# Carried sums of a grouped softmax kept in PSUM: the carry is multiplied bank to bank, and a ninth identity product goes

## The reference

```python
w_m = (efeat @ W_msg + b_msg).reshape(E, in_f, -1)
w_a = (efeat @ W_attn + b_attn).reshape(E, in_f, -1)
h_src = feat[src][:, :, None]
e1 = w_m * h_src                       # values, 16 x 16 an edge
e2 = w_a * h_src                       # scores, 16 x 16 an edge
seg_max = jax.ops.segment_max(e2, dst, num_segments=N)
ex = jnp.exp(e2 - seg_max[dst])
denom = jax.ops.segment_sum(ex, dst, num_segments=N)
ft = jax.ops.segment_sum(e1 * (ex / denom[dst]), dst, num_segments=N)
return ft.sum(axis=1)                  # then residual and layer norm
```

## Time and profile before

| | |
|---|---|
| median of 3 runs | 5913.23 us (5909.15 to 5915.31) |
| the profiled execution's own time | 5915.26 us |
| its span, first to last instruction | 5913.5 us |
| VectorE busy over the span | 5183.5 us (88%) |
| TensorE, GpSimd, ScalarE busy | 4496.4 (76%), 4372.5 (74%), 2455.9 us (42%) |
| granted TensorE clock, mean of the span | 0.899 |

### The profile page before, as it was taken

One profiled execution on the slowest core, in us unless ns is written; L12 is line 12 of the kernel. 1 busy time (PEld: TensorE's weight loads), 2 busy tenths in 40 slices (PEclk: granted clock), 3 DMA queues, 4 the chain that ended last, 5 costly groups with the idle time before them and its releaser, 6 DMA issues. The chain is left out here.

```text
span 5913.5 us, 71022 instructions
## 1 busy us (share of the span) xinstructions
PE 4496.4 (76%) x17923; PEld 2168.9 (37%) x17923; DVE 5183.5 (88%) x8909; ACT 2455.9 (42%) x4460; POOL 4372.5 (74%) x4105
## 2 busy tenths in 40 slices
PE   1178887887878878678888888888888888888880
PEld 1044444444444444333333333333333333333330
DVE  5378787787877878699999999999999999999996
ACT  1022222222222222155555555555555555555553
POOL 6677777777777777277777777777777777777762
PEclk6599999999999999889999999999999999989995
DMA  4133333333333333111111111111111111111113
GB/s 134 47 92 92 96 96 93 99 92 94 87 77 77 76 78 76 30 26 27 27 27 27 27 27 27 27 27 27 26 26 27 27 27 27 27 27 27 27 21 114
DMA packets 335266, 315.22 MB, mean 53 GB/s; under 512 B 190903, under 2 KB 274576, under 8 KB 334977
## 3 DMA queue, kind: packets, MB, share of 16 engines
q0 software_dynamic: 156096, 199.34, 14.9%
q1 hardware_dynamic: 179137, 115.52, 7.2%
HBM read 220.82 MB, written 168.57 MB: 66 GB/s over the span
## 5 line engine op out<-in xcount | busy, mean ns | idle before, releaser
L1020 POOL DMA_INDIRECT xg<-x1tab,edge x1920 | 1976.2, 1029 | 585.2 <-issue 583.7
L787 PE MATMUL pagg<-ohh,stt 128*128 128x512 bf16 x4704 | 1702.6, 401 | 458.9 <-DVE ohh L707 458.7
L654 POOL DMA_INDIRECT bg<-btab,mt x1568 | 1683.2, 1073 | 479.6 <-issue 476.3
L1091 PE MATMUL ps<-work,ident 128*128 128x512 f32 x3840 | 1942.7, 630 | 0.2 <-DVE work L1179 0.2
L788 PE MATMUL pagg<-ohh,stt 128*128 128x270 bf16 x4704 | 1370.9, 291 | 0.0
L1140 DVE TENSOR_TENSOR work<-pw,xg 128x1024 f32<-128x1024 f32 x960 | 1112.5, 1210 | 21.3 <-DMA xg<-x1tab,edge 21.3
L1080 PE MATMUL pw<-w,et 99*128 99x512 bf16 x1920 | 680.1, 441 | 574.3 <-DVE work L1140 568.5
L1091 PEld LDWEIGHTS ps<-work,ident 128*128 128x128 f32 x3840 | 779.6, 203 | 725.4 <-issue 632.3
L1063 ACT ACTIVATE work<-work,mt 128x256 f32<-128x256 f32 x1920 | 861.5, 500 | 131.3 <-DVE work L1140 109.2
L787 PEld LDWEIGHTS pagg<-ohh,stt 128*128 128x128 bf16 x4704 | 481.5, 102 | 1140.6 <-DVE ohh L707 535.6
L750 ACT CAST joined<-rest 128x256 bf16<-128x256 f32 x196 | 79.7, 407 | 1572.6 <-DVE rest L677 1572.6
(11 more groups left out here) (232 smaller groups left out, 3780.5 us busy)
## 6 DMA issues: line engine op xcount, KB each, us to landing
etab<-joined SPq DMA_DIRECT2D x389, 102.0 KB, 2.3
xg<-x1tab,edge POOLq DMA_INDIRECT x1920, 2.4
bg<-btab,mt POOLq DMA_INDIRECT x1568
rtab<-zrow SPq DMA_DIRECT2D x56, 384.0 KB, 3.3
tab<-rtab SPq DMA_DIRECT2D x7, 2048.0 KB, 8.3
e<-in_edge_attr_dram SPq DMA_DIRECT2D x392, 32.0 KB, 2.1
e<-in_edge_attr_dram SPq DMA_DIRECT2D x392, 16.0 KB
mt<-meta SPq DMA_DIRECT2D x240, 6.0 KB
```

The source lines that it names most:

```text
L654: g.indirect_dma_start(bg[:, h, i, :], None, btab, bass.IndirectOffsetOnAxis(ap=mt[:, h, 0, i:i + 1], axis=0)).then_inc(gathered[h], 16)
L787: pe.matmul(pagg[:, 0, :], w, ohh[:, h, i, 0:CUT], start=False, stop=False, skip_group_check=True)
L1020: g.indirect_dma_start(xg[:, b % 4, i, :], None, x1tab, bass.IndirectOffsetOnAxis(ap=edge[:, b, i, EW - 1:EW], axis=0)).then_inc(x_in[b % ...
L1091: pe.matmul(ps[:, b % 2, :], ident[:, :], work[:, b % 4, i, :, :, :].rearrange("p i a o -> p (i a o)"), start=i == 0, stop=False)
```

## The change

The tile `carry` in SBUF and the ninth product go. At the start two products write zeros into both `ps` banks. From then on the eight products of a tile all add to what is in their bank (`start=False`), and `carry_on(n)` prepares that: VectorE reads the finished sums of tile n-1 from the one bank, multiplies them by `corr` of tile n, and writes them into the other. It has moved: in VectorE's body it now stands between the two halves of `products(n)`, and it is for tile n, not n-1. It waits for `summed` (tile n-1's products done) and for the copy of tile n-2 (which frees the bank that it writes). TensorE's first product of a tile now waits for `carried` in place of `st_done`. ScalarE's copy of a finished bank, other than the last, waits for `carried` of the next tile in place of `summed`, so that it does not read the bank together with VectorE.

```diff
-            carry = tsb("carry", [GP, 2, 2 * C])
...
+            ps_zeroed = sem("l1_ps_zeroed")
...
                     if at := tile(t, q, -1):
                         n, b, r = at
-                        act.wait_ge(summed, n + 1)
+                        if isinstance(n, int) and n == NT - 1:
+                            act.wait_ge(summed, n + 1)
+                        else:
+                            act.wait_ge(carried, n + 2)
                         act.copy(state[:, b, C:3 * C], ps[:, b % 2, :]).then_inc(st_done, 1)
...
                 pe.wait_ge(primed, 1)
+                for h in range(2):
+                    ins = pe.matmul(ps[:, h, :], ident[:, :], state[:, U - 1, C:3 * C], start=True, stop=True)
+                ins.then_inc(ps_zeroed, 1)
...
                         if i == 0:
 
-                            wait(pe, st_done, n - 1)
+                            pe.wait_ge(carried, n + 1)
                         if i % H == 0:
                             pe.wait_ge(p_done, 2 * n + i // H + 1)
-                        pe.matmul(ps[:, b % 2, :], ident[:, :], work[:, b % 4, i, :, :, :].rearrange("p i a o -> p (i a o)"),
-                                  start=i == 0, stop=False)
+                        return pe.matmul(ps[:, b % 2, :], ident[:, :], work[:, b % 4, i, :, :, :].rearrange("p i a o -> p (i a o)"),
+                                         start=False, stop=i == J - 1, skip_group_check=True)
...
                     if done:
-                        total(done, J - 1)
-                        n, b, r = done
-                        pe.wait_ge(carried, n + 1)
-                        pe.matmul(ps[:, b % 2, :], ident[:, :], carry[:, b % 2, :], start=False, stop=True).then_inc(summed, 1)
+                        total(done, J - 1).then_inc(summed, 1)
...
                 v.sem_inc(w_used, 2)
+                v.wait_ge(ps_zeroed, 1)
...
                     v.wait_ge(corr_done, n + 1)
-                    wait(v, st_done, n)
-                    v.tensor_tensor(channels(carry[:, b % 2, :], 2), channels(state[:, (b - 1) % U, C:3 * C], 2),
+                    wait(v, summed, n)
+                    wait(v, st_done, n - 1)
+                    v.tensor_tensor(channels(ps[:, b % 2, :], 2), channels(ps[:, (b - 1) % 2, :], 2),
                                     channels(corr[:, b % 4, :]).unsqueeze(2).to_broadcast([GP, D, 2, D]),
                                     ALU.mult).then_inc(carried, 1)
...
                     if now:
                         maxima(now)
-                    if last := tile(t, q, -1):
-                        carry_on(last)
                     if ahead:
                         v.wait_ge(x_in[ahead[1] % 4], 16 * J * (2 * ahead[2] + ahead[1] // 4 + 1))
                         for i in range(0, J, 2):
                             edges(ahead, i)
                     if now:
-                        for half in range(2):
-                            products(now, half)
-
-                rounds(v, body, 1, 1)
+                        products(now, 0)
+                        carry_on(now)
+                        products(now, 1)
+
+                rounds(v, body, 1, 0)
```

## The result

The changed kernel takes 6570.43 us (median, 6568.78 to 6573.88, 4 runs) where the kernel before takes 5912.81 (5909.15 to 5915.31, 4 runs). The ratio is 1.1116, with a 95% interval of 1.1101 to 1.1131: it is slower by 658 us. The forecast was 6386, with a range of 6085 to 6560. The direction and the wait that causes the loss were forecast rightly; the size of that wait was too small, and the time lies 10 us above the range.

The account below looks back on a forecast made before the run. VectorE was taken as the bound. From 5915.3 us: -1 (ninth product's end), +1 (carry's duration), +473 (carry's wait, 239 x 1.98) gave 6388, named 6386 for the median; range 6085 to 6560 us.

Parts of the forecast that it names:

- The bound and the mechanism: Edge stage: VectorE is the bound; the moved carry waits for total 7, and the whole wait is added to the tile.
- The chain at full clock, 0.73 us: Carry's wait at full clock: total 7 done at 4023.75, first half of the products issued by 4023.02, so 0.73 us.
- full clock throughout: Rival for the edge stage: the wait stays 0.73 us in every tile, 6089 us; chance 0.14, including near it.
- The clock falls in more tiles: TensorE, idle 3.5 us in every tile, gets the low clock in more tiles; carry's wait 1.98 us, +473 us.
- the middle, 1.98: Carry's mean wait in us, taken between 1.56 with today's mix of tiles and 2.39 with every tile slow.
- with every tile a slow one 2.39: Carry's wait in a slow tile, 2 x 1.56 - 0.73 us, assuming about one tile in two waits 0.73 today.
- Slow in most of the chain, 3.06 us, 6646 us: Rival: low clock covers more of TensorE's chain from edges to total 7, every tile; wait 3.06 us, 6646 us; chance 0.10.
- TensorE's idle time, 3.5 us: Ahead of TensorE's weights: idle 3.5 us in every tile, against 2.72 in about every second one today.
- The carry's duration: VectorE's carry with PSUM input: 5 ns longer than its 678 ns, +1 us in all; bounds 0 and +45 ns.
- The ninth product, 0: Removing TensorE's ninth product, 204 us of its work, gains 0 in the loop and 1 us at the stage's end.
- The other waits, 0: TensorE's first total, ScalarE's copy and the GpSimd scatter and gathers behind it: later waits cost 0.
- GpSimd paces: Rival: GpSimd is the true pacer, hidden VectorE slack absorbs the carry's wait, time stays 5914 us; chance 0.04.

Follow-up runs that it names:

- a2: Changed kernel with identity products 5 and 6 issued with the first five, product 7 behind the second edge instruction's weights: 5899.8 us, 0.9977 of the kernel before.
- a3: Changed kernel with one more float32 identity product, of zeros, ahead of product 7: 6704.9 us, 1.1339 of the kernel before.
- a1: Changed kernel with ten bf16 products of zeros behind the transposes, in TensorE's idle time: 6089.6 us, 1.0300 of the kernel before.
- b1: Kernel before with a tenth product, of zeros, ahead of the ninth: 5939.7 us, 1.0039 of the kernel before.
- a4: Changed kernel with a2's early products, plus two second-half products moved between the next tile's chained maxima on VectorE: 5849.7 us, 0.9893 of the kernel before.

## Why the prediction was right and wrong

- *The bound and the mechanism.* Right. VectorE had no free time, the carry waits for product 7, and the whole wait falls on the tile. Shown by a2 (the wait gone by moving TensorE's products alone) and by a3 (one product more, 0.8 us more of wait).
- *The chain at full clock, 0.73 us.* Right: 0.75 in a1, whose 6089.6 us is the 6089 of the rival "full clock throughout". That the two agree to 1 us is luck; the waits of a1 are 181 us in all, where 174 were counted.
- *The clock falls in more tiles.* Right in direction; the size of this term is the step that failed. The prediction took "the middle, 1.98" between today's mix, 1.56, and "with every tile a slow one 2.39". Measured is 2.72. Of the 0.74 us between, 0.41 is the halving: all 238 tiles with 3.1 us or more of idle time ahead of the chain ran part of it at the low clock, and but for the first two and the last two carries no wait was under 1.7 us, so tiles at full clock, which the middle needs, do not occur. The other 0.33 is the price of a slow tile: 2.39 came from the mean, on the assumption that exactly half of the tiles were slow, and one tile with 2.43 seemed to confirm it. The trace of before, counted tile by tile in the prediction's way, has 128 tiles of 234 at full clock and 106 with the low clock in their chain, which imply waits of 1.7 to 3.7 us, 2.58 on average, 35 of them over 3. The long wait of 4.8 in the earlier trace rows, which gives 3.74, said that slower tiles exist. (2.72 - 1.98) x 239 = 177 us, which is the miss of 184 but for 7.
- *Slow in most of the chain, 3.06 us, 6646 us.* This rival, with a chance of 0.10, was 76 us off, nearer than the forecast. What spoke against it, that a slower chain raises TensorE's share, didn't bring the clock back: behind a slow chain VectorE waits too, and the next idle time of TensorE is again 3.1 us. Before, TensorE was late behind a slow tile and VectorE was not, so the next idle time was short: the tile behind each of these 106 had 1.7 us or less, and all but one of them ran their chains at full clock. The change took away this balance. The prediction had said so (each tile starts from the same point), and still halved the effect.
- *TensorE's idle time, 3.5 us.* Measured 3.1. TensorE's first product starts 0.93 us behind the end of product 7, where 0.6 and 0.1 were counted, and its work up to the transposes' end takes 5.0 and not 4.9; VectorE's side, 9.05 us, was counted right at 9.1.
- *The carry's duration.* 700 ns behind a wait in the changed kernel, 689 without one (a2); 5 ns were taken, 22 and 11 measured, inside the bound of 45. By the Trainium skill, "VectorE: DVE Perf Modes", section on the TRN2 errata, it would be an estimated 65 ns more for the input in PSUM; no run here shows that much.
- *The ninth product, 0.* Consistent with the edges' 0.0 before, and with b1, where a tenth cost 21 us and not 204. Its tail end was not separated from the rest.
- *The other waits, 0.* Right: no other VectorE group shows idle time, and ScalarE's copy starts 0.03 us behind the carry.
- *GpSimd paces.* Refuted: 3.5 us of free time a tile after, and in a4 13.26 us a tile without any wait of VectorE. (The rows add up to 774.9 us busy, not 774.7, which changes nothing.)

## What to carry to other kernels

Before an instruction of the bounding engine is made to wait for another engine, find the last point at which that engine was released by the first, and count both paths from there; the difference is paid in every turn of the loop. If that other engine is TensorE, count its path at the low clock too wherever it stands idle ahead of it, and read the slow turns one by one in place of halving a mean: here nearly every turn had the same 3.1 us of idle time and a low clock in its chain, and the waits still ran from 1.7 to 3.4 us. The cure was to issue, in the idle time, all that doesn't need the late release, so that the awaited product ends early; the same change then gained 0.2%, and with two chained gaps filled 1.1% (a2 and a4).

## What the runs showed of the hardware

- TensorE is faster with more work: ten products of zeros in its idle time of 3.1 us a tile took the granted clock of the stage from 0.83 to 1.00 and 481 us off the kernel (a1).
- GpSimd's gathers show no idle time but 0.30 us of "issue" ahead of each, in tiles of 13.26, 13.43 and 13.5 us alike. Their rows stretch instead: 1030 ns on average before, 1007 in a4, and 995 in the changed kernel, where GpSimd visibly waits. A full GpSimd timeline doesn't show that it paces.
- VectorE's instructions on 512 float32 mostly start 0.60 us apart when independent (602 ns from subtraction to subtraction in a2) and some 0.1 us later when one waits for the one ahead (713 ns from the second of the maxima to the third in a2); two such gaps, filled, gave 50 us over 240 tiles (a4).
- Of the tiles of the kernel before with 2.7 us of idle time on TensorE ahead of the chain, 105 ran part of it at the low clock and 22 did not; of its 107 tiles with 1.7 us or less, one did. In the changed kernel all 238 tiles with 3.1 us or more did.
